# Router matmuls in column groups, masks in row groups, and a new order of work in a pipelined vision layer

## The reference

```python
gray  = einsum('bchw,c->bhw', x, (0.2989, 0.587, 0.114))
edge  = (|conv3x3(gray, scharr)| + |conv3x3(gray, scharr.T)|) / 2
h     = edge + attention(layernorm(edge))        # rows are tokens, T = D = 256
out   = h + experts(layernorm(h))
# attention: xk, xv, xr = mixes of x and x shifted by one token
#   k, v, r = xk @ Wk.T, xv @ Wv.T, xr @ Wr.T
#   wkv: per channel a scan over tokens with a running maximum, numerator, denominator
#   (sigmoid(r) * wkv) @ Wo.T
# experts: logits = x @ Wg.T; top1 = argmax(logits), 8 experts of width 64
#   y = sum over e of (top1 == e) * (gelu((xhat*s_e + b_e) @ W1_e + b1_e) @ W2_e + b2_e)
```

## Time and profile before

| | us |
|---|---|
| three executions: median (lowest to highest) | 1283.6 (1282.58 to 1284.55) |
| the profiled execution | 1283.62 |
| its span, first to last instruction | 1281.7 |
| busy in the span: TensorE / its weight loads | 1194.3 / 709.9 |
| VectorE / ScalarE / POOL | 1045.4 / 778.3 / 6.4 |
| mean granted TensorE clock, share of 2.4 GHz | 0.984 |

### The profile page before, as it was taken

The page is one execution under the profiler, slowest core; times in us unless marked ns, Lnnn a source line. Parts: engine busy times, 40 slices in busy tenths (PEclk is TensorE's granted clock), DMA queues, the critical chain, the costliest instruction groups (busy, mean ns, idle before and its releaser), DMA issues.

```text
span 1281.7 us, 16346 instructions
## 1 busy us (share of the span) xinstructions
PE 1194.3 (93%) x5283; PEld 709.9 (55%) x5283; DVE 1045.4 (82%) x1827; ACT 778.3 (61%) x1228; POOL 6.4 (1%) x43
## 2 busy tenths in 40 slices
PE   0477999999999999999999999999999999999998
PEld 0224555656655565565556656655565665556666
DVE  2579888898888888888888888888889888888771
ACT  0166656666666656676666657666566767566551
POOL 2000000000000000000000000000000000000000
PEclk9788999999999999999999999999999999999999
DMA  5965355434445553444455434345543434530000
GB/s 172 204 145 118 69 135 135 131 100 107 94 109 134 134 133 107 110 95 99 126 134 134 117 99 111 85 124 134 134 125 97 112 89 114 134 86 17 17 17 33
DMA packets 145236, 140.06 MB, mean 109 GB/s; under 512 B 9440, under 2 KB 145206, under 8 KB 145206
## 3 DMA queue, kind: packets, MB, share of 16 engines
q1 hardware_dynamic: 145206, 139.69, 43.1%
HBM read 105.96 MB, written 33.69 MB: 109 GB/s over the span
## 4 chain that ended last, share of the span: by engine, by line
PE 72%; DVE 19%; issue 4%; DMA 3%; SPq 1%; ACT 0%; DVEq 0%
PE bank L832 22%; PE bank L925 17%; PE bank L884 17%; PE bank L958 9%; DVE mixed_v L636 3%; DVE normed L624 3%; DVE gray L490 3%; DVE gray L494 2%; DVE rwkv L620 2%; PE bank L951 2%; PE bank L899 2%; DVE mixed_k L636 2%; PE bank L926 1%; DMA gray_dram<-gray 1%; DMA hidden<-in_L_ffn_W_dram 1%
## 5 line engine op out<-in xcount | busy, mean ns | idle before, releaser
L884 PE MATMUL bank<-normed_t,w_t 128*128 128x512 f32 x512 | 242.5, 596 | 0.0
L925 PE MATMUL bank<-w_sb,hidden 128*128 128x256 f32 x1024 | 237.2, 379 | 0.8 <-ACT hidden L732 0.8
L925 PEld LDWEIGHTS bank<-w_sb,hidden 128*128 128x128 f32 x1024 | 186.9, 190 | 47.1 <-issue 14.4
L832 PE MATMUL bank<-mixed_k,w_k_t 128*128 128x512 f32 x256 | 130.7, 637 | 26.4 <-DVE rank L512 15.9
L851 PE MATMUL bank<-rows_in,conv_w 102*32 102x512 f32 x1024 | 122.1, 619 | 25.5 <-issue 19.9
L780 ACT ACTIVATE v_sb<-bank 128x512 f32<-128x512 f32 x64 | 37.6, 587 | 175.5 <-PE bank L832 175.5
L884 PEld LDWEIGHTS bank<-normed_t,w_t 128*128 128x128 f32 x512 | 94.7, 190 | 78.8 <-issue 71.8
L832 PE MATMUL bank<-mixed_r,w_r_t 128*128 128x512 f32 x256 | 122.8, 603 | 5.5 <-DVE mixed_r L636 5.5
L958 PE MATMUL bank<-w_o_t,rwkv 128*128 128x256 f32 x512 | 115.8, 379 | 0.2 <-DVE rwkv L620 0.2
L832 PE MATMUL bank<-mixed_v,w_v_t 128*128 128x512 f32 x256 | 115.1, 592 | 0.0
L958 PEld LDWEIGHTS bank<-w_o_t,rwkv 128*128 128x128 f32 x512 | 97.2, 190 | 26.7 <-issue 14.8
(11 more groups left out here) (118 smaller groups left out, 1821.6 us busy)
## 6 DMA issues: line engine op xcount, KB each, us to landing
planes<-in_x_dram SPq DMA_DIRECT2D x64, 768.0 KB, 6.3
rows_in<-gray_dram SPq DMA_DIRECT2D x192, 256.0 KB
gray_dram<-gray SPq DMA_DIRECT2D x64, 258.0 KB, 2.7
out_dram<-edge SPq DMA_DIRECT2D x64, 256.0 KB, 2.2
rows_in<-gray_dram SPq DMA_DIRECT2D x128, 24.0 KB
hidden<-in_L_ffn_W_dram SPq DMA_DIRECT2D x2, 256.0 KB, 9.2
w_sb<-in_L_ffn_W_dram SPq DMA_DIRECT2D x1, 512.0 KB, 4.6
gate<-in_L_attn_Wk_dram SPq DMA_DIRECT2D x1, 256.0 KB, 5.9
```

What stands on the lines that cost most here:

```text
L832: ins = pe.matmul(dst[:, :], w_t[i][:, kt, ct * P:(ct + 1) * P], mixed[i][:, 2 * kt:2 * kt + 2, :].rearrange("p i t -> p (i t)"), start=(k ...
L884: pe.matmul(ps[:, :], w1_t[:, kt, m * P:(m + 1) * P], normed2_t[:, kt, :, :].rearrange("p i t -> p (i t)"), start=(kt == 0), stop=False)
L925: pe.matmul(ps, hidden[:, m, i, rows], w2_sb[:, m, :], start=(m == 0), stop=False)
```

## The change

Logits: `wg_t` is padded to 32 columns and becomes the weight, the tokens move; each block of 128 tokens goes to its own column group of one bank, so the logits come out transposed. ScalarE copies them (`copy_logits`), TensorE transposes them back at the start of the next step (`transpose_logits`). Masks: the route is written four times instead of three times and its complement, and part m of the hidden layer uses rows 32m to 32m+31 only. POOL builds the mask rows accordingly, in eight selections and a scaling. The banks are dealt out anew. `step_diff`, `abs_a` and two more `resid` buffers get memory of their own; the result is written over `resid`. Waits for a count of zero are left out (`wait`). `rwkv`, the reciprocal and v's mix move to the next step. Each engine has a new order.

```diff
-        BANK_EDGE, BANK_WO, BANK_K, BANK_V, BANK_R = (0, 1, 2, 3), (4, 5), (6, 7), (0, 1), (7, 0)
-        BANK_W = (5, 6, 7, 4)
-        BANK_HIDDEN, BANK_NORMED2, BANK_Y, BANK_NORMED = (3, 4, 5, 6), (1, 2), (3, 4), (5, 6)
+        BANK_EDGE, BANK_WO, BANK_K, BANK_V, BANK_R = (3, 5, 1, 2), (0, 1), (7, 1), (4, 1), (3, 2)
+        BANK_HIDDEN, BANK_NORMED2, BANK_Y, BANK_NORMED = (4, 6, 7, 5), (4, 7), (3, 0), (7, 4)
+        BANK_LOGITS_T, BANK_LOGITS, BANK_ROUTE, BANK_W = 6, 4, 5, (4, 6, 7, 0)
...
+            for g in range(NM):
+                rows = slice(32 * g, 32 * (g + 1))
+                pool.affine_select(out=mask_rows[rows, :], in_=mask_rows[rows, :], compare_op=ALU.is_ge, fill=0.0,
+                                   base=0, pattern=[[1, E * H]], channel_multiplier=-H).then_inc(s_cleared, 1)
...
+            pool.tensor_scalar(mask_rows[:, :], mask_rows[:, :], -1.0, MASK_OUT, ALU.mult, ALU.add
+                               ).then_inc(s_cleared, 1)
```

VectorE's new order:

```diff
+            def step(at):
+                mix(1, WKV, s_mix_v, at)
+                best_hits(at)
+                gated_wkv(at)
+                rank_hits(at)
+                running_max(0, at)
+                first_hit(at)
+                gap_of(0, at)
+                running_max(1, at)
+                route_of(at)
+                gap_of(1, at)
+                gray_of(at)
+                residual(0, at)
+                edge_sum(0, at)
+                residual(1, at)
+                resid_stats(at)
...
+                edge_sum(1, at)
+                aggregate(1, PROJ, at)
+                edge_stats(at)
...
+                mix(2, WKV, s_mix_r, at)
+                aggregate(0, EDGE, at)
+                den_scan(at)
+                normalise2(at)
+                fresh_values(at)
+                edge_shift(at)
+                denominator(at)
+                num_scan(at)
+                bonus_values(at)
+                result(0, at)
+                numerator(at)
+                step_difference(at)
+                gate_numerator(at)
+                mix(0, EDGE, s_mix_k, at)
+                result(1, at)
+                best_logit(at)
```

ScalarE's new order:

```diff
+            def step(at):
...
+                log_denominator(at)
+                reciprocal(at)
+                absolute(0, at)
+                absolute(1, at)
+                absolute(2, at)
+                copy_v(0, at)
+                decay_arg(at)
+                decay_of(at)
+                absolute(3, at)
+                fresh_arg(at)
+                fresh_of(at)
+                copy_route(at)
+                bonus_arg(at)
+                reciprocal_std(1, PROJ, at)
+                bonus_of(at)
+                copy_v(1, at)
+                reciprocal_std(0, EDGE, at)
+                for m in range(NM):
+                    gelu(m, at)
+                gate_of(0, at)
+                normalise(at)
+                copy_normed2(0, at)
+                copy_normed2(1, at)
+                copy_normed(0, at)
+                copy_normed(1, at)
+                gate_of(1, at)
...
+                copy_logits(at)
```

TensorE, what its operations wait for and the new shapes:

```diff
+            def project_k(ct, at):
...
+                if ct == 0:
+                    wait(pe, s_mix_k, at.count(WKV, 1, 1))
+                else:
+                    wait(pe, s_abs, at.count(WKV, 4, 3, back=-1))
+                project(0, ct, bank[BANK_K[ct]], s_k_ps)
...
+            def project_v(ct, at):
...
+                if ct == 0:
+                    wait(pe, s_mix_v, at.count(WKV, 1, 1))
+                    wait(pe, s_hits, at.count(WKV, 1, 1, back=2))
+                else:
+                    wait(pe, s_gap, at.count(WKV, 2, 2))
+                    wait(pe, s_resid, at.count(WKV, 2, 2, back=1))
+                project(1, ct, bank[BANK_V[ct]], s_v_ps)
...
+            def mask_out(at):
...
+                wait(pe, s_route_t, at.count(FFN, 1, 1))
+                for m in range(NM):
+                    rows = slice(32 * m, 32 * (m + 1))
+                    ins = pe.matmul(bank[BANK_HIDDEN[m]][:, :], mask_rows[rows, m * P:(m + 1) * P],
+                                    route_t[rows, :, :].rearrange("p i t -> p (i t)"),
+                                    start=(m == NM - 1), stop=(m < NM - 1))
+                ins.then_inc(s_masked, 1)
...
+            def route_logits(at):
...
+                wait(pe, s_normed2_t, at.count(PROJ, 2, 2))
+                for kt in range(CH):
+                    for half in range(HALF):
+                        for i in range(2):
+                            q = 2 * half + i
+                            ins = pe.matmul(bank[BANK_LOGITS_T][32 * q:32 * (q + 1), 0:P], wg_t[:, kt, :],
+                                            normed2_t[:, kt, i, half * P:(half + 1) * P],
+                                            start=(kt == 0), stop=(kt == CH - 1))
+                ins.then_inc(s_logits_ps, 1)
...
+            def transpose_logits(at):
...
+                wait(pe, s_logits_t, at.count(FFN, 1, 1))
+                pe.transpose(bank[BANK_LOGITS][:, 0:P], logits_t[:, :], ident[:, :]).then_inc(s_logits, 1)
...
+            def second_layer(half, at):
...
+                if half == 0:
+                    wait(pe, s_gate, at.count(FFN, 2, 1, back=-2))
+                    wait(pe, s_hidden, at.count(FFN, 4, 4))
```

TensorE's new order:

```diff
+            def step(at):
+                transpose_logits(at)
+                convolve(0, at)
+                convolve(1, at)
+                convolve(2, at)
+                project_k(0, at)
+                project_k(1, at)
+                project_v(0, at)
+                output_projection(0, at)
+                transpose_route(at)
+                convolve(3, at)
+                output_projection(1, at)
+                first_layer(0, at)
+                first_layer(1, at)
+                first_layer(2, at)
+                mask_out(at)
+                project_v(1, at)
+                project_r(0, at)
+                first_layer(3, at)
+                project_r(1, at)
+                transpose_normed2(0, at)
+                transpose_normed2(1, at)
+                second_layer(0, at)
+                transpose_normed(0, at)
+                transpose_normed(1, at)
+                route_logits(at)
+                second_layer(1, at)
```

More of the change, by code:

```diff
@@ L828, in before_experts, with convolve @@
                 pe.wait_ge(s_cleared, CLEARED_MASK)
-            def project(at, i, ct, dst):
+            def convolve(n, at):
+                if not at.has(EDGE):
+                    return
+                half, c = divmod(n, 2)
+                if n == 0:
+                    wait(pe, s_rows_loaded, at.count(EDGE, 16 * X_DMAS, 16 * X_DMAS))
+                    wait(pe, s_result, at.count(EDGE, 2, 1, back=4))
+                for q in range(4):
+                    rows = rows_in[0:TAPS, 4 * half + q, :, :].rearrange("p i w -> p (i w)")
+                    ins = pe.matmul(bank[BANK_EDGE[n]][ROW_TILE * q:ROW_TILE * (q + 1), :],
+                                    conv_w[0:TAPS, c, :], rows, start=True, stop=True)
+                ins.then_inc(s_edge_ps, 1)
@@ new lines, in project_v, with project_r @@
+            def project_v(ct, at):
+                if not at.has(WKV):
+                    return
+                if ct == 0:
[5 more added lines that the diff above has]
+                project(1, ct, bank[BANK_V[ct]], s_v_ps)
+            def project_r(ct, at):
+                if not at.has(WKV):
+                    return
+                if ct == 0:
+                    wait(pe, s_mix_r, at.count(WKV, 1, 1))
+                else:
+                    wait(pe, s_abs, at.count(WKV, 4, 4, back=-1))
+                project(2, ct, bank[BANK_R[ct]], s_r_ps)
@@ L956, in output_projection @@
+            def output_projection(half, at):
+                if not at.has(PROJ):
+                    return
+                if half == 0:
+                    wait(pe, s_rwkv, at.count(PROJ, 1, 1))
+                else:
+                    wait(pe, s_gap, at.count(PROJ, 2, 2, back=-1))
                 for i in range(2):
@@ new lines, in transposed, with transpose_normed2 @@
+            def transposed(src, ps, ct):
+                for i in range(2):
+                    for half in range(HALF):
+                        col = i * T + half * P
+                        ins = pe.transpose(ps[:, col:col + P], src[:, 2 * half + i, ct * P:(ct + 1) * P], ident[:, :])
+                return ins
+            def transpose_normed2(ct, at):
+                if not at.has(PROJ):
+                    return
+                if ct == 0:
+                    wait(pe, s_hidden, at.count(PROJ, 4, 1, back=1))
+                    wait(pe, s_normed2, at.count(PROJ, 1, 1))
+                else:
+                    wait(pe, s_hidden, at.count(PROJ, 4, 3, back=1))
+                transposed(normed2, bank[BANK_NORMED2[ct]], ct).then_inc(s_normed2_ps, 1)
```

748 lines of the change are left out of this document (354 added, 394 removed).

## The result

The new kernel's median is 1233.1 us (1232.1 to 1234.9, four executions) against 1283.1 (1281.2 to 1284.6) for the kernel before on the same chip: a ratio of 0.9613, 95% interval 0.9596 to 0.9630. The forecast was 1227, the range 1214 to 1250. The profiled execution took 1234.9, its span is 1233.2.

The account below looks back on a forecast made before the run. TensorE was taken as the bound, with one hole of 0.86 us a step; 37.15 becomes 35.29. Fill -3.5, 26 steps of 1.86 (-48.4) and -4.9 give -56.8 against 1283.6: 1227 us, range 1214 to 1250.

Parts of the forecast that it names:

- the fill: Start of the run: the sixth step's k at 129.3, the next step at 161.6 instead of 165.13, -3.5 us.
- hole and restart: TensorE's wait before k's second half closes: -0.86 us a step, and -0.07 for the restart.
- logits, with copy back and trip: TensorE's logits in four column groups: 1.78 us becomes 0.48, plus 0.22 for transposing back and 0.19 for the trip.
- masks, with trip: TensorE's four mask passes in four row groups: 0.86 us a step becomes 0.38, plus 0.19 for the trip.
- convolution 3 by itself: Convolution 3, moved behind the route transposes on TensorE, needs its own trip: +0.19 us a step.
- a trip: One change of TensorE's array grouping and back: 0.19 us, 0.06 in and 0.13 out; three more a step, +0.57.
- The setup: POOL's extra mask work ends near 13 instead of 8.15; nothing lost, at most 4 us.
- The covers: Slack hiding the new waits, costed at nothing: v 3.8 us, ScalarE's gate 0.3 before the second layer, VectorE 0.3 to 1.0.
- A: Rival: groups overlap badly on TensorE, logits 0.91, masks 0.6, a trip 0.3; +1.0 us a step, 1254; chance 0.12.
- B: Rival: a new hole as ScalarE's or VectorE's margin turns negative by 0.4 to 0.8 a step; 1238 to 1250; chance 0.14.
- D: Rival: the hole isn't closed, as v or the projection waits instead; 0.9 us more, 1252; chance 0.02.
- C: Rival: slower, no grouping overlaps and each change drains the array; decides from 0.24 a trip, 1314 at 0.6; chance 0.04.

Follow-up runs that it names:

- hole alone: Kernel before, with VectorE's maximum and comparison of the logits moved ahead of gray, TensorE's order unchanged: 1261.5 us, ratio 0.9825.
- old form: New kernel with the logits as before (tokens as weights, eight moving columns, no copy or transposition back): 1263.5 us, ratio 0.9842.
- all rows: New kernel with the four mask matmuls over all 128 rows instead of 32 rows each, so no row grouping: 1246.1 us, ratio 0.9701.
- joined: New kernel with convolution 3 directly behind convolution 2, with its own wait on the gate: 1227.6 us, ratio 0.9572.
- the run with one row group: New kernel with all four mask matmuls in rows 0 to 31, so they can't overlap but the change of grouping stays: 1257.3 us, ratio 0.9790.
- the logits beside the convolutions: New kernel with convolution 3 behind convolution 2 and the logits at the step's end, next to the following step's convolutions: 1215.7 us, ratio 0.9470.
- The variant with gray first: New kernel with gray as VectorE's first work in steps 0 to 4 only: 1231.6 us, ratio 0.9603.
- the new kernel again: The new kernel unchanged, executed again to measure the spread: 1236.5 us, ratio 0.9630.

## Why the prediction was right, and which terms were off

The mechanism held: a TensorE step with one hole, which the new order closes, and two shapes made narrow and set side by side. The steady part was forecast to give 48.4 and gave 43.9, the drain 4.9 and gave 4.5, the fill 3.5 and gave 0.1; together 48.5 of span instead of 56.8.

| a step, us | forecast | measured | by |
|---|---|---|---|
| hole and restart | -0.93 | -0.83 | hole alone |
| logits, with copy back and trip | -0.83 | -0.83 | old form: -0.91, of which 0.08 was no cost before |
| masks, with trip | -0.29 | -0.34 | all rows |
| convolution 3 by itself | +0.19 | +0.28 | joined |
| sum | -1.86 | -1.72 | the step: -1.70 |

- **The step that was wrong in the sum: "I take the measured 0.19" for a trip.** What I had measured was the way in, 0.06, and the way out, 0.13. The third part, 0.10 in the first group behind, was in the rows as well: k's first half behind the convolutions. But its slot also held the hole, and I gave all of 2.58 - 1.72 to the hole. That made the hole 0.10 too big and each trip 0.10 too small. The hole-alone run tells them apart, and three comparisons give 0.28 to 0.30. The trip of the logits looks dearer by its slots, 0.10 + 0.14 + 0.10 = 0.34 (the transposes ahead 0.97 instead of 0.87, the way out, the group behind 1.83 instead of 1.73); no run isolates it.
- **Logits and masks.** The groups overlap fully: less the way out, which is 0.14 for convolution 3 and 0.10 in the run with one row group, the slots of 0.57 and 0.32 leave 0.43 and 0.22 of streaming, the least I had allowed, where I took 0.48 and 0.38. The 0.46 of the logits beside the convolutions shows the first of them directly. The transposition back adds one pass of 0.11 and not two: 0.20 to the convolutions, of which 0.09 is the way in. These better terms, 0.05 + 0.16 + 0.11 = 0.32 a step, hid two thirds of the 0.48 by which the hole and the trips came out worse than forecast; so far the nearness of 35.29 to 35.45 is luck.
- **What row groups gain, and what a change costs.** The four masks take 0.22 by themselves, a quarter (1/3.9) of the 0.86 before, but 0.52 with their trip, which is a gain of 1.65x only: in this kernel the trip decides what they are worth. The Trainium skill (TensorE: Matmul & The Clock Gate, Measured speedup vs the span model) gives 3.07x for four row groups; by it the masks would cost 0.28, more than the runs show without the trip and less than with it. A trip costs 0.28 to 0.30 on both sides of the change, half of a full pass of 592 ns. The Trainium skill (TensorEngine Tiling (Array Packing), Key Properties) says that a change of tiling mode drains the array; the runs agree that a change costs, and do not show whether the array is empty in between.
- **The fill: the other step that failed.** "My count has k at 129.3 and the next step at 161.6" took the rows of the fourth step to be there when TensorE came. In the new order gray stands there behind the running maxima, SP writes it at 79.72, and TensorE waits 5.77 for rows. In the steady part the last of the loads are issued at 644.35 for convolutions at 661.6, and the same move costs nothing; in the fill there is no such slack. The variant with gray first gives 3.3 back, nearly the 3.5 forecast.
- **The setup** held: POOL's last instruction starts at 12.46. The border writes wait for it (issued at 13.00 instead of 8.55), but SP, which waits for them to land, goes on at 16.86, not later than the 17.16 before; the first convolution starts at 39.07, before 39.59.
- **The drain** held within half a microsecond: steps of 35.45, 30.94 and 22.85, and 1.77 of waiting for the route in the last one.
- **The range.** The sum of the least case in "How the numbers follow" is 0.48 and not 0.44 (0.05 for the logits, 0.16 for the masks, 3 x 0.09 for the trips); 1214 stays, rounded.
- **The covers** held. VectorE idles at the three places named, and the gate has 0.6 instead of 0.3 before the second layer, since it took ScalarE 5.44 from the end of v's slot (646.35) and not 5.75, against the same 6.03 of TensorE.
- **Rivals.** A (groups overlap badly) falls by 0.43 and 0.22, though its dear trip of 0.3 was right; by itself that added 3 x 0.10 a step. B (a new hole) and D (the hole stays) fall by a TensorE that is busy for 35.45 of 35.45. C's condition, a trip from 0.24 on, was met and it still didn't come about, because it also needed groups without overlap; the run with the masks in one group shows that case in small, where tiling without overlap loses 0.30 a step against none.

What stays open: why the clock of the fill differs between executions of the same kernel. One waits 2.33 just ahead of the convolutions at 129.82 and runs them at 2.4 GHz, the other waits 1.84 ahead of those at 129.68 and runs them at 1.2. The lower level had set in earlier there, at the transposes of `normed` behind a longer wait, as the two timelines of TensorE show, the new kernel first and then the new kernel again:

```profile
125.59 1.09 PE L1034 MATMUL bank<-ident,normed 128*128 128x128 f32 x8 [1.75 <-ACT normed_t L839]
```

```profile
124.86 1.59 PE L1034 MATMUL bank<-ident,normed 128*128 128x128 f32 x8 [3.18 <-ACT normed_t L839]
```

But that wait does not decide it either: the variant with all masks in one row group waits 1.75 there, as the first does, and still takes 5.35 for its three convolutions.

## What to carry to other kernels

Read the price of a change of grouping on both sides of it, from the group before to the first group behind, and compare each with the same shape elsewhere; a slot that also holds a wait hides part of it. Put work of the same grouping side by side, which here held for 128 and 102 rows: two trips less, with the transposition in a better place, were worth 0.62 us a step here, nearly twice what tiling the masks gave. And look at a moved producer in the fill by itself, since there its consumers have no slack.

## What the runs showed of the hardware

- Four column groups of 128 moving f32 columns each stream in the time of one: sixteen matmul instructions with their sixteen weight loads in 0.43 to 0.46, under 0.03 each, where the closest pairs of load and matmul in the kernel before were 0.057 apart.
- Going from 128-row to 102-row weights in the same four column groups costs 0.03 at most (0.46 against 0.43), while a change from the whole array to column groups or to row groups costs 0.28 to 0.30 for the way there and back. No run goes from column groups to row groups directly.
- At the two ends, where TensorE had waited for 1.75 to 3.18 us, the granted clock was in one execution at its lower level (5.35 for three convolutions, 3.48 for half of the output projection) and in another at the upper (2.78 and 1.84), which moved the time by about 4.
